# Two layers of attention and expert feed-forward on one core: the last layer norm of the first attention stage is finished by the next stage, and the end of the rotary attention runs in another order

## The chip, the cores and the metric

One core of one Trainium2 chip runs the whole program. The core has five engines that run side by side, each with its own instruction queue: PE (matrix products), DVE and POOL (elementwise work), ACT (activation functions and copies) and SP (which here only issues DMA transfers). They meet through semaphores. The metric is device time in microseconds, from one launch to its end; lower is better.

## The reference, cut to what matters

```python
# x: (8, 256, 256), context: (8, 256, 256)
x = x + tanh(g_xattn[0]) * L0_attention(layernorm(x), context)
x = x + tanh(g_ffn[0])   * L0_experts(layernorm(x))                 # 8 experts, the best 2 of each row
x = x + tanh(g_xattn[1]) * L1_rotary_attention(layernorm(x), context)
x = x + tanh(g_ffn[1])   * L1_experts(layernorm(x))                 # 8 experts, the best 1 of each row

def L0_attention(x, enc):
    x2 = layer_norm(x  + mha(x,  x,   x),   ln1_g, ln1_b)
    x4 = layer_norm(x2 + mha(x2, enc, enc), ln2_g, ln2_b)           # "the last norm of the attention"
    x5 = relu(x4 @ ff_w1 + ff_b1) @ ff_w2 + ff_b2
    return layer_norm(x4 + x5, ln3_g, ln3_b)
```

A layer norm here is (row - mean) / sqrt(variance + 1e-5), then times a gain and plus a shift of 256 numbers each. An expert layer sends each row to its expert (`relu(x @ W1[e] + b1[e]) @ W2[e] + b2[e]`) and weights the answer with the router's softmax.

## The kernel before

Rows are kept as 8 sequences of 256 rows, each as two tiles of 128 rows on 128 partitions. `X` holds the running value and `Y` the normed one; `here(Y, n)` is sequence n of it.

The program is a chain of stages. Each is a block in which every engine has a queue of its own, written out by hand; between two blocks all engines meet at a barrier (`stage_semaphores`), so a stage starts when the last engine of the one before is done. The stages that matter:

1. `attention_pipeline` (names `att_`): both attentions of layer 0 as one pipeline of M = 16 units, unit m being sequence m % 8 of the first attention for m < 8 and of the second for m >= 8. It runs in beats b, and a beat has 16 heads h. In beat b the heads of unit b are worked on; the output product of unit b - 1 (`project_out`, into `att_z`) comes at h = 12, and the layer norm of unit b - 2 is spread over the beat. So after the last unit's heads there are two more beats, b = 16 and b = 17, that hold only output products and norms. For the norm of unit m, DVE adds the product to `att_ybb` (`output_rows`) and takes mean and variance (`row_stats`), POOL finds the inverse root by 14 tiny instructions in a chain (`inverse_roots`), DVE scales (`norm`), and POOL multiplies with the gain and adds the shift (`gain_and_shift`). `att_ybb` is the residual plus the product's bias, made on POOL (`add_bias`). On POOL a beat is: roots, gain and shift of unit b - 2, then the bias of unit b - 1.
2. `feed_forward_and_experts` (`moe_`): the small feed-forward with its norm over 8 sequences, n = 0 to 7, and then 39 slots of 128 rows, each for one expert. PE runs `turn` (transposes of sequence n), `up_bank`, `down`. SP loads three rows of parameters first (`moe_b2r`, `moe_gain`, `moe_shift`), then the weights of 8 experts, 16 transfers of 1 MB.
3. `rotary_and_experts` (`out_`): the second layer's attention, in beats of 16 heads again (M = 8), then 23 slots of 128 rows for the experts with the best one of 8. The first 4 slots (`EARLY`) are filled from the first 6 sequences alone. For that the router works on a sequence as soon as it is normed: PE turns it (`turn_router`, task "t"), ACT copies it (`bring_router`), PE makes the logits (`logits`, "l"), DVE picks the expert (`top_expert`), PE counts ranks (`rank`, "n"), DVE makes destinations and weights, and POOL scatters the row numbers to DRAM (`scatter`, `ids<-out_numbered`). Then SP reads the list of a slot (`numbers`, `out_ids<-ids`), POOL gathers its rows (`rows_in`, `X<-rows` and `Y<-rows`), and PE turns and multiplies them (`turn_slot`, `up_slot` L1326, `down_slot` L1339). SP also writes each normed sequence to DRAM for these gathers (`keep_rows`), and `load_expert` loads 2 MB of an expert's weights; those of experts 6 and 7 need the place of the attention's operands.

Two of the PSUM banks of stage 3 are shared by all small products. `rotary_banks` gives the tasks the banks in turn, in the order in which PE meets them, and a task waits until the task two places before it has been read out. The end of the stage's attention, behind the last beat, is called the drain.

## Time and profile before

| | us |
|---|---|
| median of 3 runs | 1419.33 |
| lowest, highest | 1418.34, 1425.44 |
| the profiled execution's own time | 1420.58 |
| its span, first to last instruction | 1418.7 |
| PE busy in it | 1217.6 (86%) |
| DVE, ACT, POOL busy | 771.6, 560.9, 503.2 |

Times in the trace count from the first instruction of the span. The attention stage of layer 0 ends at about 466 us, the feed-forward stage runs from there to about 917 us, and the rotary stage to the end; its attention ends at about 1230 us. PE is the engine that is busy most, so the question at each place is what PE waits for.

### The profile page before, as it was taken

The page shows a single profiled execution, that of the slowest core. Times are in us where ns is not written, and L with a number is a line of the kernel's source. Part 1 is how long each engine was busy: PE and PEld are TensorE (multiplying, and loading weights), DVE is VectorE, ACT ScalarE, POOL GpSimd, SP SyncE. Part 2 cuts the span into 40 slices and gives each one's busy share as a digit, 9 for nine tenths or more (in the row PEclk, how much of TensorE's full clock was granted, in tenths as well). Part 3 has the DMA queues.
Part 4 walks back from the last instruction along what each step waited for, and adds up shares of the span by engine and source line. Part 5 has one row for each costly group of instructions (what it writes and reads, how often), then busy time and mean ns, then how long its engine had stood idle before and what let it go on. Part 6 is the DMA issues. An engine that isn't in the chain of part 4 may idle for free. (4 is left out here: it accounts for less than half of the span.)

```text
span 1418.7 us, 27157 instructions
## 1 busy us (share of the span) xinstructions
PE 1217.6 (86%) x8465; PEld 972.0 (69%) x8520; DVE 771.6 (54%) x2819; ACT 560.9 (40%) x1349; POOL 503.2 (35%) x909
## 2 busy tenths in 40 slices
PE   4598989999996899898999999755687888589996
PEld 3376666777753688788889888633455555489995
DVE  4676766777772277853412121147787876443321
ACT  2265555666664222233233333211354546133331
POOL 3344444453534235421000000156765543333331
PEclk9799999999999899999999999966799989799998
DMA  5767885657520771111111010166455587511110
GB/s 118 172 154 189 205 200 143 152 154 159 143 63 1 272 259 42 38 46 46 34 35 38 31 38 31 57 151 140 112 136 106 95 275 230 177 32 39 44 33 7
DMA packets 126293, 155.92 MB, mean 110 GB/s; under 512 B 19499, under 2 KB 111801, under 8 KB 121276
## 3 DMA queue, kind: packets, MB, share of 16 engines
q1 hardware_dynamic: 113736, 122.68, 34.2%
q0 software_dynamic: 9792, 27.30, 6.1%
q10 hardware_dynamic: 2624, 4.19, 1.0%
q8 instruction: 72, 1.18, 0.4%
q14 instruction: 69, 0.57, 0.2%
HBM read 104.17 MB, written 52.32 MB: 110 GB/s over the span
## 5 line engine op out<-in xcount | busy, mean ns | idle before, releaser
L761 DVE CUSTOM_DVE_ANT_0 att_masked_scores<-att_S,Bm 128x256 bf16<-128x256 f32 x512 | 192.4, 419 | 71.7 <-PE att_S L507 59.3
L644 ACT ACTIVATE att_PT<-att_T 128x512 f32<-128x512 f32 x256 | 151.4, 595 | 99.5 <-PE att_T L526 90.6
L2419 ACT ACTIVATE moe_hT<-moe_H,moe_b 128x128 f32<-128x128 f32 x312 | 89.2, 369 | 195.5 <-PE moe_H L2334 194.2
L2334 PE MATMUL moe_H<-moe_aT,ff_w 128*128 128x128 f32 x1248 | 147.7, 277 | 8.4 <-DVE ff_w L2617 8.4
L2334 PEld LDWEIGHTS moe_H<-moe_aT,ff_w 128*128 128x128 f32 x1248 | 146.7, 194 | 11.7 <-DVE ff_w L2617 9.9
L2346 PE MATMUL moe_Z<-moe_W,moe_hT 128*128 x624 | 142.6, 381 | 0.8 <-DVE moe_z L2624 0.8
L1615 POOL DMA_INDIRECT L_W<-yd,dest x32 | 31.3, 979 | 279.8 <-POOLq L52 271.2
L2346 PEld LDWEIGHTS moe_Z<-moe_W,moe_hT 128*128 128x128 f32 x624 | 115.4, 190 | 15.5 <-issue 1.2
L2624 DVE TENSOR_TENSOR moe_z<-moe_Z,moe_b 128x256 f32<-128x256 f32 x39 | 16.5, 424 | 200.7 <-PE moe_Z L2346 200.7
L507 PE MATMUL att_S<-L_KS,L_QS 96*128 96x256 bf16 x512 | 99.8, 277 | 26.9 <-DMA L_KS<-att_k_dram 21.7
L526 PE MATMUL att_T<-L_QS,L_KS 99*128 99x256 bf16 x512 | 98.7, 273 | 4.8 <-issue 2.3
L1790 DVE TENSOR_REDUCE out_mx<-out_S 128x2 f32<-128x512 f32 x128 | 85.8, 684 | 16.7 <-PE out_S L1207 11.8
L1507 ACT ACTIVATE X<-out_T,L_b 128x128 f32<-128x128 f32 x184 | 52.4, 370 | 97.5 <-PE out_T L1326 96.5
L1326 PEld LDWEIGHTS out_T<-out_xT,L_w1s 128*128 128x128 f32 x736 | 86.5, 194 | 4.4 <-issue 1.8
L1326 PE MATMUL out_T<-out_xT,L_w1s 128*128 128x128 f32 x736 | 87.3, 277 | 2.6 <-DVE L_w1s L1943 1.4
L1473 ACT ACTIVATE L_W<-out_T 128x512 f32<-128x512 f32 x128 | 72.5, 596 | 38.1 <-PE out_T L1225 31.9
L1339 PE MATMUL out_S<-L_W,X 128*128 x368 | 83.5, 380 | 2.5 <-DVE out_ys L1952 2.5
L524 PE MATMUL att_T<-BmT,identb 128*128 128x512 bf16 x201 | 77.0, 383 | 0.4
L526 PEld LDWEIGHTS att_T<-L_QS,L_KS 99*128 99x128 bf16 x512 | 50.6, 99 | 38.8 <-issue 0.8
L1207 PE MATMUL out_S<-L_W 97*128 97x256 bf16 x256 | 55.3, 305 | 25.2 <-DVE out_mx L1790 22.0
L1339 PEld LDWEIGHTS out_S<-L_W,X 128*128 128x128 f32 x368 | 68.1, 190 | 11.8 <-issue 3.5
L507 PEld LDWEIGHTS att_S<-L_KS,L_QS 96*128 96x128 bf16 x512 | 48.0, 98 | 40.6 <-DMA L_KS<-att_k_dram 23.2
(460 smaller groups left out, 2384.4 us busy)
## 6 DMA issues: line engine op xcount, KB each, us to landing
moe_W<-in_L_ffn_W SPq DMA_DIRECT2D x16, 1024.0 KB, 13.6
xd<-zero SPq DMA_DIRECT2D x12, 1280.0 KB
L_W<-in_L_ffn_W POOLq DMA_DIRECT2D x12, 1024.0 KB, 9.3
att_q_dram<-att_pq SPq DMA_DIRECT2D x16, 384.0 KB
att_k_dram<-att_pk SPq DMA_DIRECT2D x16, 384.0 KB
L_QS<-att_q_dram SPq DMA_DIRECT2D x16, 384.0 KB
L_KS<-att_k_dram SPq DMA_DIRECT2D x16, 384.0 KB
moe_xs<-xd SPq DMA_DIRECT2D x39, 128.0 KB
```

Source lines behind the costliest of these rows:

```text
L507: ins = nc.tensor.matmul(bankS[h % 2][:, u * SEQ:(u + 1) * SEQ], QS[0:ROWS, m % 3, h, u * P:(u + 1) * P], KS[0:ROWS, m % 3, h, :], start=T ...
L524: nc.tensor.matmul(dst[:, :], identb[:, :], masks[m // B][1][:, :], start=True, stop=False)
L526: ins = nc.tensor.matmul(dst[:, u * SEQ:(u + 1) * SEQ], KS[0:ROWS_ALL, m % 3, h, u * P:(u + 1) * P], QS[0:ROWS_ALL, m % 3, h, :], start=Fa ...
L644: nc.scalar.activation(PT[:, h % 8, :], bankT[h % 2][:, :], ACT.Exp).then_inc(exp_done, 1)
L761: ins = nc.vector.tensor_tensor_reduce(masked_scores[:, h % 2, u, :], bankS[h % 2][:, u * SEQ:(u + 1) * SEQ], masks[m // B][0][:, u * SEQ: ...
L1326: ins = nc.tensor.matmul(bankH[half][:, f * P:(f + 1) * P], matrix[:, cc, k * P:(k + 1) * P], xT[:, s % 2, cc * P:(cc + 1) * P], start=(cc ...
L1339: ins = nc.tensor.matmul(bankY[:, 0:D], eT[:, s % 2, f * P:(f + 1) * P], matrix[:, f, :], start=(f == 0), stop=(f == NF - 1))
L1473: nc.scalar.activation(PT[h % 8], bankT[h % 2][:, :], ACT.Exp).then_inc(exp_done, 1)
L1790: nc.vector.tensor_reduce(mx[:, m % 2, :, h:h + 1], bankS[h % 2][:, :].rearrange("p (u k) -> p u k", u=NU), AXX, ALU.max).then_inc(max_don ...
L2334: ins = nc.tensor.matmul(bankH[half][:, f * P:(f + 1) * P], w1s[:, cc, g * P:(g + 1) * P], xT[:, s % 2, cc * P:(cc + 1) * P], start=(cc == ...
L2346: ins = nc.tensor.matmul(bankZ[:, 0:D], eT[:, s % 2, f * P:(f + 1) * P], w2e[:, f, :], start=(f == 0), stop=(f == NF - 1))
L2419: ins = nc.scalar.activation(eT[:, s % 2, g * P:(g + 1) * P], bankH[half][:, f * P:(f + 1) * P], ACT.Relu, bias=b1[:, bass.ds(e * NF + g, 1)])
```

## The change

In `attention_pipeline` the beats stop after b = 16. The norm of the last unit (m = 15, sequence 7) isn't done there: DVE adds product and residual straight into `Y`, and the rest of the norm moves to the start of `feed_forward_and_experts`. In beat 16 POOL does the bias of unit 15 before the roots of unit 14. The feed-forward stage norms sequence 7 with its own helpers (`norm_rows` on DVE with the square root on ACT, whose function table is loaded for it) and a new `finish_last` on POOL; gain and shift come by two more transfers on SP, ahead of the others, into `yT`. Later readers of that sequence or of `yT` wait for `last_done`.

In `rotary_and_experts` the router's steps for sequence 5, the last of the early ones, move from the drain into the last beat; the drain's order changes on PE, DVE and POOL; and the loads of experts 6 and 7 move from ACT's queue to SP's, behind the four early lists.

```diff
@@ attention_pipeline
-        BEATS = range(-4, M + 2)
+        BEATS = range(-4, M + 1)
+        normed_here = lambda m: 0 <= m < M - 1
@@ POOL
+                if b == M:
+                    add_bias(M - 1)
-                if has(b - 2):
+                if normed_here(b - 2):
                     inverse_roots(nc, pool, t, moments, root_step, b - 2).then_inc(rooted, 1)
...
-                if has(b - 2):
+                if normed_here(b - 2):
                     gain_and_shift(b - 2)
-                if has(b - 1):
+                if has(b - 1) and b < M:
                     add_bias(b - 1)
@@ DVE, output_rows
-                nc.vector.tensor_tensor(z[:, m % 2, :, :], bank_of("z", m)[:, :].rearrange("p (u d) -> p u d", u=NU), ybb[:, :, :],
+                dst = z[:, m % 2, :, :] if m < M - 1 else here(Y, m)
+                nc.vector.tensor_tensor(dst, bank_of("z", m)[:, :].rearrange("p (u d) -> p u d", u=NU), ybb[:, :, :],
@@ rotary_tasks
+    more = LAST_BEAT.get(h, ()) if b == B - 1 else ()
...
-DRAIN_TASKS = ("t", 5), ("l", 5), ("o", 31), ("n", 5), ("a", 7), ("z", 7), ("t", 6), ("l", 6), ("t", 7), ("l", 7), ("n", 6), ("n", 7)
+LAST_BEAT = {11: (("t", 5),), 14: (("l", 5),)}
+DRAIN_TASKS = ("n", 5), ("o", 31), ("a", 7), ("z", 7), ("t", 6), ("l", 6), ("t", 7), ("l", 7), ("n", 6), ("n", 7)
@@ rotary_and_experts, SP
-            keep_rows(B - 2)
             sp.wait_ge(early_made, 1)
             sp.wait_ge(scattered[0], 16 * NU * EARLY_ONES)
             for s in range(EARLY):
                 numbers(s)
+            keep_rows(B - 2)
+            sp.wait_ge(s_ready, ALL)
+            sp.wait_ge(st_ready, ALL)
+            load_expert(sp, NE - 2)
+            sp.wait_ge(pv_done, QUADS * M + 2)
+            load_expert(sp, NE - 1)
             experts_here(NE - 2, NE)
@@ PE
+                    if b == M - 1 and h == 11:
+                        turn_router(EARLY_ONES - 1)
...
+                    if b == M - 1 and h == 14:
+                        logits(EARLY_ONES - 1)
...
-            turn_router(EARLY_ONES - 1)
             values(QUADS * M - 1)
-            logits(EARLY_ONES - 1)
+            rank(EARLY_ONES - 1)
             turn_out(QUADS * M - 1)
-            rank(EARLY_ONES - 1)
@@ ACT
+                    if b == M - 1 and h == 12:
+                        bring_router(EARLY_ONES - 1)
...
-            bring_router(EARLY_ONES - 1)
-            act.wait_ge(s_ready, ALL)
-            act.wait_ge(st_ready, ALL)
-            load_expert(act, NE - 2)
             outputs(QUADS * M - 1)
-            act.wait_ge(pv_done, QUADS * M + 2)
-            load_expert(act, NE - 1)
@@ POOL
+            scatter(EARLY_ONES - 1)
             inverse_roots(nc, pool, t, moments, root_step, M - 2).then_inc(rooted, 1)
-            scatter(EARLY_ONES - 1)
+            rows_in(0)
             inverse_roots(nc, pool, t, moments, root_step, M - 1).then_inc(rooted, 1)
-            for s in range(EARLY):
+            for s in range(1, EARLY):
                 rows_in(s)
@@ DVE
+                    if b == M - 1 and h == 15:
+                        top_expert(EARLY_ONES - 1)
+                        centre(EARLY_ONES - 1)
...
             row_stats(M - 2)
-            top_expert(EARLY_ONES - 1)
-            centre(EARLY_ONES - 1)
+            destinations(EARLY_ONES - 1)
             normalise(QUADS * M - 1)
-            destinations(EARLY_ONES - 1)
             expert_weights(EARLY_ONES - 1)
             early_table()
+            output_rows(M - 1)
             norm(M - 2)
-            output_rows(M - 1)
@@ feed_forward_and_experts
+            for i, k in enumerate(("last_gain", "last_shift")):
+                sp.dma_start(yT[:, i, :], rows_in[k].partition_broadcast(P)).then_inc(last_in, 16)
@@ turn(n)
+                if n == B - 1:
+                    pe.wait_ge(last_done, 1)
@@ bring_router(n)
+                if n == 0:
+                    act.wait_ge(last_done, 1)
@@ ACT
             bring(0)
+            norm_root(nc, act, t1, step1, root1, 0)
@@ POOL
+            def finish_last():
+                pool.wait_ge(last_in, 32)
+                pool.wait_ge(last_normed, 1)
+                nc.gpsimd.tensor_tensor(here(Y, B - 1), here(Y, B - 1), rows_of(yT[:, 0, :]), ALU.mult).then_inc(last_scaled, 1)
+                pool.wait_ge(last_scaled, 1)
+                nc.gpsimd.tensor_tensor(here(Y, B - 1), here(Y, B - 1), rows_of(yT[:, 1, :]), ALU.add).then_inc(last_done, 1)
...
             add_bias(0)
+            finish_last()
@@ DVE
+            norm_rows(nc, dve, here(Y, B - 1), here(Y, B - 1), t1, step1, root1, 0, waited).then_inc(last_normed, 1)
             then(routing_constants(nc, rt))
```

The first place is POOL's queue where the attention stage of layer 0 ends. Before, behind gain and shift of unit 14 (`att_z`, `Y`), it held this:

```order
L711 TENSOR_TENSOR att_z<-att_z,L_gain 128x512
L713 TENSOR_TENSOR Y<-att_z,L_shift 128x512
L707 TENSOR_TENSOR att_ybb<-Y,L_bo 128x512
L134 TENSOR_SCALAR att_ve<-att_mv 128x2
L135 TENSOR_SCALAR att_guess<-att_ve 128x2
L138 TENSOR_TENSOR att_a<-att_guess 128x2
L139 TENSOR_TENSOR att_b<-att_a,att_ve 128x2
L140 TENSOR_SCALAR att_c<-att_b 128x2
L141 TENSOR_TENSOR att_r<-att_guess,att_c 128x2
```

Now the block's end (the branch) follows at once, and the new work stands behind the first bias of the next stage; `moe_yT` holds the gain and then the shift of the last unit:

```order
L712 TENSOR_TENSOR att_z<-att_z,L_gain 128x512
L714 TENSOR_TENSOR Y<-att_z,L_shift 128x512
L346 UNCONDITIONAL_BRANCH
L51 ISA x2
L2475 UNCONDITIONAL_BRANCH
L2502 IOTA moe_slot_no 1x27
L2479 TENSOR_TENSOR Y<-Y,moe_b2r 128x512
L2484 TENSOR_TENSOR Y<-Y,moe_yT 128x512
L2486 TENSOR_TENSOR Y<-Y,moe_yT 128x512
```

What went from POOL's end of the stage is the bias of unit 15 (it stands earlier now), its 14 root instructions and its gain and shift.

The second place is PE's queue from head 11 of the last rotary beat. L1225 are the transposed scores of a head (`out_T`), L1238 the values of four heads (`out_O`), L1246 turns of their outputs, L1267 the output product of sequence 6, L1277 the router's turn and L1289 its logits. Before:

```order
L1246 MATMUL out_B<-ident,out_OTS 128x128 x2
L1225 MATMUL out_T<-L_W 128x256 x2
L1267 MATMUL out_A<-L_wo,out_aT 128x256 x4
L1225 MATMUL out_T<-L_W 128x256 x2
L1238 MATMUL out_O<-L_W,L_w1s 32x256 x8
L1225 MATMUL out_T<-L_W 128x256 x4
L1246 MATMUL out_B<-ident,out_OTS 128x128 x2
L1277 MATMUL out_A<-ident,Y 128x128 x4
L1238 MATMUL out_O<-L_W,L_w1s 32x256 x8
L1289 MATMUL out_B<-L_wg,out_yT 128x8 x4
```

And of the change, where these lines are 11 higher:

```order
L1288 MATMUL out_B<-ident,Y 128x128 x4
L1257 MATMUL out_A<-ident,out_OTS 128x128 x2
L1236 MATMUL out_T<-L_W 128x256 x2
L1278 MATMUL out_B<-L_wo,out_aT 128x256 x4
L1236 MATMUL out_T<-L_W 128x256 x2
L1249 MATMUL out_O<-L_W,L_w1s 32x256 x8
L1236 MATMUL out_T<-L_W 128x256 x2
L1300 MATMUL out_A<-L_wg,out_yT 128x8 x4
L1236 MATMUL out_T<-L_W 128x256 x2
L1257 MATMUL out_B<-ident,out_OTS 128x128 x2
L1249 MATMUL out_O<-L_W,L_w1s 32x256 x8
```

The router's turn stands ahead of the output product now, and both write bank B, so the product waits until ACT has copied the turned rows; the logits stand ahead of the last values.

The third place is SP's queue behind the fourth early list (`out_ids<-ids`). Before, only sequence 7 was written to DRAM there (`rows<-Y`, `rows<-X`) ahead of the later lists. Now it is this, with sequence 6, four weight transfers of 1 MB and then sequence 7:

```order
L1102 DMA out_ids<-ids 128x2
L1091 DMA rows<-Y 128x2x256
L1091 DMA rows<-X 128x2x256
L1053 DMA L_W<-in_L_ffn_W 128x2x1024
L1054 DMA L_W<-in_L_ffn_W 128x8x256
L1053 DMA L_W<-in_L_ffn_W 128x2x1024
L1054 DMA L_W<-in_L_ffn_W 128x8x256
L1091 DMA rows<-Y 128x2x256
L1091 DMA rows<-X 128x2x256
```

What moved here is the rows of sequence 6, which stood ahead of the lists, and the weights, which stood on ACT.

## Rows read from the trace of the kernel before

**Rows 1.** The page's head.
```profile
span 1418.7 us, 27157 instructions
```
**Rows 2.** Timeline of PE at the end of layer 0's attention: start us, us, group.
```profile
450.68 1.99 PE L568 MATMUL att_B<-L_wo,att_aT 128*128 128x256 f32 x8 [0.75 <-ACT att_aT L618]
467.07 1.09 PE L2257 MATMUL moe_T<-ident,Y 128*128 128x128 f32 x4 [14.39 <-PEq L52]
468.90 8.85 PE L2269 MATMUL moe_H<-moe_aT,ff_w 128*128 128x256 f32 x32 [0.75 <-ACT moe_aT L2389]
...
484.94 7.07 PE L2269 MATMUL moe_H<-moe_aT,ff_w 128*128 128x256 f32 x32
```
**Rows 3.** Timeline of POOL over the same stretch.
```profile
447.72 0.21 POOL L134 TENSOR_SCALAR att_ve<-att_mv 128x2 f32<-128x2 f32 x1 [4.85 <-DVE att_mv L118]
...
451.34 0.20 POOL L141 TENSOR_TENSOR att_r<-att_r,att_c 128x2 f32<-128x2 f32 x1
...
453.74 1.26 POOL L713 TENSOR_TENSOR Y<-att_z,L_shift 128x512 f32<-128x512 f32 x1
...
464.28 1.26 POOL L713 TENSOR_TENSOR Y<-att_z,L_shift 128x512 f32<-128x512 f32 x1
467.05 0.17 POOL L2476 IOTA moe_slot_no<- 1x27 f32 x1 [1.51 <-POOLq L52]
472.71 1.27 POOL L2460 TENSOR_TENSOR Y<-Y,moe_b2r 128x512 f32<-128x512 f32 x1 [5.50 <-DMA moe_shift<-in_L_xattn_ln_b]
```
**Rows 4.** Timeline of DVE over the same stretch.
```profile
443.46 0.69 DVE L802 TENSOR_TENSOR att_z<-att_B,att_ybb 128x512 f32<-128x512 f32 x1 [1.72 <-PE att_B L568]
...
456.42 0.69 DVE L802 TENSOR_TENSOR att_z<-att_B,att_ybb 128x512 f32<-128x512 f32 x1 [4.10 <-POOL att_ybb L707]
...
485.32 0.69 DVE L2508 TENSOR_TENSOR moe_z<-moe_Z,Y 128x512 f32<-128x512 f32 x1 [17.25 <-PE moe_Z L2282]
```
**Rows 5.** Busy time by stretch; the number behind POOL's is PE's granted clock.
```profile
455.00:455.50 0.50, 0.00 (x0) 0.00 (x0) 0.00 (x0) 0.00 (x0) 0.50 (x1) 0.77 0.00 0
...
472.00:472.50 0.50, 0.50 (x3) 0.42 (x2) 0.00 (x0) 0.00 (x0) 0.00 (x0) 0.66 0.88 248
```
**Rows 6.** Timeline of ACT: its first copy for the feed-forward stage's router.
```profile
499.83 0.60 ACT L2404 ACTIVATE moe_yT<-moe_R 128x512 f32<-128x512 f32 x1 [2.75 <-PE moe_R L2292]
```
**Rows 7.** Chain that ended last, in the rotary drain: start us, us, what.
```profile
1205.25 1.00 PE out_B L1289 x8
...
1210.57 1.03 POOL ids L1635
...
1211.90 7.30 DMA ids<-out_numbered,out_place
...
1220.21 3.21 DMA out_ids<-ids
...
1224.25 4.06 DMA X<-rows,out_ids
1228.36 0.69 PE out_S L1311 x2
...
1231.50 4.59 PE out_T L1326 x32
```
**Rows 8.** Timeline of PE in the last rotary beat and behind it.
```profile
1199.57 1.89 PE L1267 MATMUL out_A<-L_wo,out_aT 128*128 128x256 f32 x8
...
1204.18 1.07 PE L1238 MATMUL out_O<-L_W,L_w1s 128*32 128x256 f32 x16
```
**Rows 9.** Timeline of ACT in that beat: the exponentials of heads 10 to 12.
```profile
1198.69 1.68 ACT L1473 ACTIVATE L_W<-out_T 128x512 f32<-128x512 f32 x3
```
**Rows 10.** DMA issues of 1184 to 1197 us: transfers, median us to landing.
```profile
ids<-out_numbered,out_place POOLq DMA_INDIRECT x2, 4.6
```
**Rows 11.** DMA issues of 1198 to 1209 us, in the same columns.
```profile
L_W<-in_L_ffn_W ACTq DMA_DIRECT2D x4, 1024.0 KB, 11.7
```
**Rows 12.** Timeline of POOL: the gather of slot 4.
```profile
1256.40 1.28 POOL L1649 DMA_INDIRECT X<-rows,out_ids  x1 [3.30 <-DMA out<-X,out_ids]
```

More of the change, by code:

```diff
@@ L831, in _ @@
                         queries(b + 3)
-                    if h == 1 and has(b - 2):
+                    if h == 1 and normed_here(b - 2):
                         row_stats(b - 2)
@@ L841, in _ @@
                         max_columns(b + 1)
-                    if h == 9 and has(b - 2):
+                    if h == 9 and normed_here(b - 2):
                         norm(b - 2)
@@ L870, in rotary_tasks @@
         return [t for t in LAST_FILL.get(h, ())]
+    more = LAST_BEAT.get(h, ()) if b == B - 1 else ()
     units = [(k, QUADS * b + d if k == "o" else b + d) for k, d in TASKS.get(h, ()) + ROUTE_TASKS.get(h, ())]
     last = {"o": QUADS * B, "t": EARLY_SEQUENCES1 - 1, "l": EARLY_SEQUENCES1 - 1, "n": EARLY_SEQUENCES1 - 1}
-    return [(k, n) for k, n in units if 0 <= n < last.get(k, B)]
+    return more + tuple((k, n) for k, n in units if 0 <= n < last.get(k, B))
 ROUTE_TASKS = {1: (("l", -3),), 5: (("n", -3),), 13: (("t", -2),)}
-DRAIN_TASKS = ("t", 5), ("l", 5), ("o", 31), ("n", 5), ("a", 7), ("z", 7), ("t", 6), ("l", 6), ("t", 7), ("l", 7), ("n", 6), ("n", 7)
+LAST_BEAT = {11: (("t", 5),), 14: (("l", 5),)}
+DRAIN_TASKS = ("n", 5), ("o", 31), ("a", 7), ("z", 7), ("t", 6), ("l", 6), ("t", 7), ("l", 7), ("n", 6), ("n", 7)
 def rotary_banks():
@@ L2212, in feed_forward_and_experts @@
         w1_ready, x_loaded, y_stored = sem("w1_ready"), sem("x_loaded"), pair("y_stored")
+        last_in, last_normed, last_scaled, last_done = sem("last_in"), sem("last_normed"), sem("last_scaled"), sem("last_done")
         block = ctx.enter_context(nc.Block())
@@ L2429, in _ @@
                 if n >= 1:
-                    norm_root(nc, act, t1, step1, root1, n - 1)
+                    norm_root(nc, act, t1, step1, root1, n)
                 for j in range(1, HB):
@@ L2440, in _ @@
             bring_router(B - 2)
-            norm_root(nc, act, t1, step1, root1, B - 1)
+            norm_root(nc, act, t1, step1, root1, B)
             for s in range(SLOTS):
@@ L2509, in rows @@
                 dve.wait_ge(z_out, n + 1)
-                norm_rows(nc, dve, z, z, t1, step1, root1, n, waited).then_inc(normed, 1)
+                norm_rows(nc, dve, z, z, t1, step1, root1, n + 1, waited).then_inc(normed, 1)
             def new_rows(n):
@@ L2708, in flamingo @@
             feed_forward_and_experts(nc, "moe", c, ff, {"b2r": a["L0_xattn_ff_b2"], "gain": a["L0_xattn_ln3_g"],
-                                     "shift": a["L0_xattn_ln3_b"]}, X, Y, L, xd0, yd0, dest, weight, gate_x0, gate_f0,
+                                     "shift": a["L0_xattn_ln3_b"],
+                                     "last_gain": a["L0_xattn_ln2_g"], "last_shift": a["L0_xattn_ln2_b"]}, X, Y, L, xd0, yd0, dest, weight, gate_x0, gate_f0,
                                      a["L0_ffn_W1"], a["L0_ffn_W2"], a["c_L0_ffn_b1"], a["L0_ffn_b2"])
```

## The prediction

> **What bounds the kernel now.** I read three views: the timelines of PE, POOL and DVE where the first attention stage ends, the chain that ended last in the rotary drain, and the sizes of DMA landings beside both. The span is 1418.7 us [rows 1]; the sum below is made against the profiled execution's own 1420.58 us, which is 1.25 above the median of 1419.33.
>
> At the first place PE is through with the attention at 450.68 + 1.99 = 452.67 and starts again at 467.07, after 14.39 us of nothing [rows 2]. The reader should see who is last: POOL, whose gain and shift of unit 15 end at 464.28 + 1.26 = 465.54, and 1.5 us later every engine is in the next stage [rows 3]. Behind 467.07 PE works without a gap through the feed-forward's sequences, so what the barrier gives up, the whole rest of the program gets, as long as the next stage's start is not made slower.
>
> At the second place the chain shows a row of handovers with PE idle: logits at 1205.25, scatter issued at 1210.57 and 1211.90, 7.30 us until it has landed, the list read by SP (3.21), the gather (4.06), PE's turn of slot 0 at 1228.36 and its first product at 1231.50 [rows 7]. From there PE is the chain to the end, so the end moves with that product.
>
> **The first part, piece by piece.** Removed from the stage's end are unit 15's statistics, 14 roots, scaling, gain and shift, and ahead of them the bias. The bias was what DVE waited for at 456.42, though the product was there at 452.67 [rows 2, 4]. Now POOL does it before the roots of unit 14. It needs the sum of unit 14, ready at 443.46 + 0.69 = 444.15 [rows 4], and takes 1.27 us; the roots of unit 14 started at 447.72 after 4.85 us of waiting [rows 3], so it hides wholly in that wait (cover 2.3 us; without it it would cost 1.27). DVE adds at about 452.7 and is done at 453.4. The last thing of the stage is then POOL's shift of unit 14, which ended at 453.74 + 1.26 = 455.00 [rows 3]; its roots (447.72 to 451.54) and what follows don't move. So the end comes at 455.00 instead of 465.54: **-10.54 us**, and PE starts at about 456.5.
>
> Added to the next stage: DVE norms sequence 7 first, some 5 us with the square root and a load of ACT's table, while it had nothing to add until 485.32, 18 us after the start [rows 4]. The table load isn't new, it stood later in the same queue. On SP two small transfers stand ahead; three such ones put POOL's first bias at 472.71, 5.6 us after the start [rows 3], so I expect it 1 to 2 us later, against those 18 us. On POOL gain and shift (2.6 us) follow the first bias, done some 11 us after the start. The first to wait for `last_done` is ACT's router copy, which came at 499.83, 32.8 us after the start [rows 6]. All this costs 0. What is queued behind it on POOL is gain and shift of sequence 0, due some 23 us after the start; if `last_done` came 22 us late, ACT, and through it PE, would wait.
>
> The clock: PE's first products in the new stage took 8.85 us where the same 32 took 7.07 later [rows 2]. The granted clock fell from 2.4 to 1.2 GHz between 455.0 and 455.5, 2.6 us after PE's last product, and rose at about 472.3 [rows 5]. PE now restarts at 456.5, still behind that fall, so I take the same price again: 0. The bounds are -2.3 us if the clock doesn't fall (8.85 - 7.07 and the same on the turns, 0.5) and +1 if it rises later.
>
> **The second part.** PE turns sequence 5 for the router at head 11, ahead of the output product. The product of sequence 6, at 1199.57 before [rows 8], now waits for ACT's copy, which comes behind the exponentials of heads 10 to 12 (1198.69 + 1.68 = 1200.37) [rows 9] and takes 0.6: it starts at about 1201.0, 1.4 us late. The logits (1.00 [rows 7]) stand ahead of the last head too. So the last values, at 1204.18 before [rows 8], come 2.4 us later. In exchange DVE picks the expert meanwhile; but now the statistics of sequence 6 and the rank behind the values stand in the way of the destinations. Going through DVE's queue, I get the weights of sequence 5 about 0.8 us later than before (bounds: 1 earlier, 2 later), and the scatter's second issue at 1212.7.
>
> Then the gain: the scatter of 1211.90 took 7.30 us to land [rows 7], in a stretch in which the 4 MB of experts 6 and 7 were arriving. The scatter before it but one took 4.6 [rows 10]. With the weights issued later I take 4.6: -2.7 (bound: 0). The list and the gather of slot 0 follow by the same steps, so its rows arrive 1.9 us earlier, at 1226.5. But POOL now does the roots of sequence 7 behind that gather, and PE wants that sequence's turn before its first slot product: roots take 3.8 us [rows 3], behind the gather's issue at 1222.3 to 1223.9, then DVE's scaling and the turn. The product starts at about 1230.4 by that path instead of 1231.3: **-0.9 us**. Bounds: -2.0 if the roots don't decide, +4 from the rival below.
>
> [...]
>
> **Sum.** 1420.58 - 10.54 - 0.9 = 1409.1 for a profiled run, 1.25 less against the median: **1408 us**, 0.8% faster.
>
> **Rivals.** (A) *The drain gives back.* The weights now leave SP at about 1222.5, just as POOL issues the gathers of slots 0 to 3 (256 KB each). The measured sign that this hurts is the scatter: 7.30 us beside such weights, 4.6 without [rows 7, 10]. A gather stretched by the same 2.7 us puts slot 0's product at 1232 and lets PE wait up to 2 more for slots 1 and 2: +3 against my sum's -0.9, so 1411.8. For it speaks that PE stands right behind; against it that the weights' bulk comes after slot 0's gather. The Trainium skill, DMA: Bandwidth & Descriptors, section on queues, rings and completion order, says each DMA engine goes round between its queues a packet at a time, which is this rival's mechanism; and under "Issuing engines are not separate DMA queues" that SP, ACT and POOL all feed the same 16 engines, by which ACT to SP alone brings nothing. By that rule slot 0's gather shares from its first packet; the scatter's row agrees in kind, and nothing before shows gathers beside weights.
>
> (B) *More than forecast.* The clock stays up over the short gap and the roots don't decide: 1419.33 - 10.5 - 2.3 - 2.0 = 1404.5. Against it is the fall at 455.0 to 455.5 [rows 5].
>
> (C) *The barrier doesn't move*, because something else than POOL ended it, or the next stage's start is late by as much (the change doesn't do what it says): 1418.4. The three rows of POOL, DVE and PE leave little room; SP's waits at the end are for transfers long done.
>
> (D) *Slower.* SP now waits until 4 MB have landed before it writes sequence 7, which slot 4's gather at 1256.40 needs [rows 12]. The loads took 11.7 us [rows 11]; from 1222.5 that is 1234, the rows landed by 1240, some 15 us in time. Only if they took over 26 us would PE wait, and only beyond 45 would it be slower than before by over 0.5%: 1427 and more.
>
> **Chances and range.** Forecast 0.58 (its own range 1405.5 to 1410.5), A 0.18, B 0.12, C 0.08, D 0.04. What a measurement of this kernel can tell from no change is about 0.5%, 7.1 us: faster is below 1412.2. The forecast, B and four fifths of A lie there, and some of C between: 0.86 faster, 0.10 same, 0.04 slower. The range 1403.5 to 1413 leaves out C, D and the far ends of A and B.
>
> **What the new profile would show.** Right: POOL's last work of the attention stage is the shift of unit 14, DVE's addition into `Y` no later than 453.5, PE's gap there near 3.9 us instead of 14.4, and the first feed-forward products again near 8.9 us. In the drain: the output product of sequence 6 behind ACT's router copy, the scatter's landing near 4.6, slot 0's turn about 13 us earlier in the trace than before (10.5 of it from the first part). Wrong: a gap on PE ahead of `turn` of sequence 7 or behind ACT's first router copy; gathers of slots 0 to 3 over 6 us to landing with PE waiting; PE waiting for weights or rows at slot 4. Most likely to make the forecast wrong is the drain, whose queues all changed at once.

## The result

| | us |
|---|---|
| median of this kernel, 8 runs (lowest, highest) | 1408.08 (1403.39, 1411.90) |
| median of the kernel before, 8 runs (lowest, highest) | 1420.23 (1416.50, 1427.94) |
| ratio, with its 95% interval | 0.9899 [0.9879, 0.992] |
| profiled execution of this kernel: own time, span | 1403.39, 1401.5 |

The kernel is 1% faster, by 12.15 us between the medians. The forecast was 1408.0 and 11.4 us of gain.

The timeline of POOL at the end of layer 0's attention in the changed kernel (start us, us, group) answers to [rows 3]:

```profile
439.81 1.27 POOL L708 TENSOR_TENSOR att_ybb<-Y,L_bo 128x512 f32<-128x512 f32 x1 [1.42 <-DVE att_z L806]
443.25 0.21 POOL L134 TENSOR_SCALAR att_ve<-att_mv 128x2 f32<-128x2 f32 x1 [2.16 <-DVE att_mv L118]
...
449.25 1.27 POOL L714 TENSOR_TENSOR Y<-att_z,L_shift 128x512 f32<-128x512 f32 x1
452.04 0.17 POOL L2502 IOTA moe_slot_no<- 1x27 f32 x1 [1.51 <-POOLq L52]
459.81 1.27 POOL L2479 TENSOR_TENSOR Y<-Y,moe_b2r 128x512 f32<-128x512 f32 x1 [7.61 <-DMA moe_shift<-in_L_xattn_ln_b]
...
462.38 1.27 POOL L2486 TENSOR_TENSOR Y<-Y,moe_yT 128x512 f32<-128x512 f32 x1
```

The bias of unit 15 stands at 439.81, inside POOL's wait for the row sums of unit 14. The shift of unit 14 is now the stage's last work, ending at 450.52, and again 1.5 us pass until POOL is in the next stage. Behind the first bias there, the two operations of `finish_last` end at 463.65.

The timeline of PE in the same stretch answers to [rows 2]:

```profile
442.10 1.07 PE L540 MATMUL att_O<-att_PT,att_V 128*32 128x256 f32 x16 [0.52 <-ACT att_PT L645]
...
446.20 3.58 PE L569 MATMUL att_B<-L_wo,att_aT 128*128 128x256 f32 x8 [0.75 <-ACT att_aT L619]
452.06 0.63 PE L2273 MATMUL moe_T<-ident,Y 128*128 128x128 f32 x4 [2.28 <-PEq L52]
453.44 8.56 PE L2285 MATMUL moe_H<-moe_aT,ff_w 128*128 128x256 f32 x32 [0.75 <-ACT moe_aT L2405]
...
462.27 7.07 PE L2298 MATMUL moe_Z<-ff_w,moe_hT 128*128 128x256 f32 x32
```

PE stands idle for 2.28 us there instead of 14.39. Its last product of the attention took 3.58 us where 1.99 in [rows 2]: the same eight matrix products at the other clock, as the busy time by stretch shows (the number behind POOL's is the granted clock, 0.50 being 1.2 GHz and 1.00 being 2.4):

```profile
447.00:449.00 2.00, 2.00 (x6) 1.55 (x6) 0.74 (x2) 0.00 (x0) 1.15 (x2) 0.50 0.00 0
450.10:452.10 2.00, 0.04 (x1) 0.07 (x2) 0.51 (x2) 0.00 (x0) 0.49 (x2) 1.00 0.00 0
453.50:456.00 2.50, 2.50 (x6) 2.05 (x7) 0.90 (x6) 1.39 (x2) 0.00 (x0) 0.50 0.47 136
460.00:462.00 2.00, 2.00 (x12) 1.72 (x11) 0.00 (x0) 0.84 (x2) 2.00 (x2) 1.00 0.95 388
```

The rows of DVE and ACT show what became of unit 15:

```profile
449.87 0.69 DVE L806 TENSOR_TENSOR Y<-att_B,att_ybb 128x512 f32<-128x512 f32 x1 [2.04 <-issue]
...
455.92 0.73 DVE L89 TENSOR_SCALAR Y<-Y,moe_amv,moe_arstd 128x256 f32<-128x256 f32 x2
...
469.56 0.69 DVE L2535 TENSOR_TENSOR moe_z<-moe_Z,Y 128x512 f32<-128x512 f32 x1 [12.45 <-PE moe_Z L2298]
```
```profile
484.07 0.60 ACT L2422 ACTIVATE moe_yT<-moe_R 128x512 f32<-128x512 f32 x1 [4.17 <-PE moe_R L2308]
```

DVE's part of the norm is done at 456.65 and then DVE waits 12.45 us for PE anyway; ACT's first router copy at 484.07 waits for PE's turn and not for `last_done`, which had come 20 us earlier.

The chain that ended last, in the rotary drain, answers to [rows 7]:

```profile
1185.28 1.96 PE out_B L1278 x8
...
1195.31 0.97 POOL ids L1644
1196.59 4.46 DMA ids<-out_numbered,out_place
1202.06 1.74 DMA out_ids<-ids
...
1204.62 5.57 DMA X<-rows,out_ids
1210.24 0.69 PE out_S L1322 x2
1210.93 1.51 PE out_B L1300 x8
1212.44 0.95 PE out_A L1288 x4
1213.38 5.57 PE out_T L1337 x32
```

The scatter lands in 4.46 us instead of 7.30, the gather in 5.57 instead of 4.06, and slot 0's turn is 18.12 us earlier in the trace than in [rows 7].

**Two marks that take the noise out.** One execution differs from the next by up to ten us, more than the drain is worth. In fourteen profiles the last value product of the attention (`att_O`, mark A) starts anywhere from 440.03 to 447.29 us, and from the second product of the feed-forward stage to the values of quad 29 (mark B, the third value product from the end of the rotary attention; 1197.26 before, 1181.52 in the changed kernel) it takes 716.2 to 722.2 us; no edit here changes PE's work in either stretch. Of the 18.12 us at slot 0's turn, 4.47 lie ahead of A (446.57 before, 442.10 in the changed kernel) and are no work of the change. Measured from A, a landmark at the barrier repeats within 0.1 us where the same engine ends the stage. Measured from B it repeats less well: the two profiles of the changed kernel (changed and e9) are 1.6 us apart at slot 0's turn and 1.3 at the end, so a single profile tells no edit of under some 1.3 us in the drain. The table has these distances in us, starts read from the timelines; "end" is the span less B. The medians come from five series; that of the kernel before was 1420.23 beside the changed kernel, 1419.84 beside e1 to e4, 1418.21 beside e5 to e8, 1417.95 beside e9 to e11 and 1418.16 beside e12, and each ratio is to the one of its own series.

| kernel | median | ratio to before | A: POOL's end | A: first turn | A: `moe_Z` | B: list | B: slot 0's turn | B: its product | B: end |
|---|---|---|---|---|---|---|---|---|---|
| before | 1420.23 | | 18.97 | 20.50 | 31.46 | 22.95 | 31.10 | 34.03 | 221.44 |
| changed | 1408.08 | 0.9899 [0.9879, 0.992] | 8.42 | 9.96 | 20.17 | 20.54 | 28.72 | 31.65 | 219.98 |
| e9, changed again | 1404.09 | 0.9899 [0.9881, 0.9917] | 8.41 | 9.95 | 20.16 | 20.29 | 27.08 | 30.01 | 218.69 |
| e1, boundary alone | 1407.73 | 0.9918 [0.989, 0.9947] | 8.39 | 9.92 | 20.80 | 22.50 | 29.70 | 32.63 | 221.21 |
| e2, drain alone | 1416.20 | 0.9979 [0.9959, 1.0] | 18.91 | 20.44 | 32.61 | 19.99 | 27.21 | 30.14 | 220.01 |
| e3, bias alone | 1417.64 | 0.999 [0.9967, 1.0012] | 16.76 | 18.29 | 29.93 | 22.51 | 29.70 | 32.63 | 221.86 |
| e4, 7 idle products | 1412.38 | 0.9952 [0.9933, 0.9972] | 17.66 | 19.19 | 30.68 | 20.13 | 27.43 | 30.36 | 219.74 |
| e10, 14 idle products | 1423.11 | 1.0045 [1.0031, 1.006] | 27.06 | 28.59 | 39.72 | 20.13 | 27.29 | 30.22 | 219.92 |
| e5, loads on ACT | 1405.77 | 0.9906 [0.989, 0.9922] | 8.44 | 10.07 | 20.35 | 23.00 | 29.59 | 32.52 | 220.94 |
| e6, router late | 1406.92 | 0.991 [0.9888, 0.9932] | 8.44 | 9.96 | 21.79 | 19.53 | 26.06 | 29.85 | 219.12 |
| e7, loads later | 1407.71 | 0.992 [0.9905, 0.9936] | 8.40 | 9.92 | 21.04 | 20.13 | 26.93 | 29.87 | 218.58 |
| e8, gather behind roots | 1410.27 | 0.9951 [0.9932, 0.997] | 8.42 | 9.95 | 21.11 | 19.91 | 34.65 | 37.59 | 224.86 |
| e11, e6 with e7 | 1401.69 | 0.9881 [0.9865, 0.9897] | 8.44 | 9.96 | 21.13 | 19.52 | 26.09 | 29.84 | 219.02 |
| e12, product first | 1401.54 | 0.9876 [0.9859, 0.9892] | 8.43 | 9.96 | 21.76 | 19.27 | 25.82 | 27.87 | 219.09 |

### The profile page after: what moved, and what is told of

It is laid out like the page before. It is cut to its first block and busy times, and to the rows that moved or that the text cites. A ratio compares the mean times of both kernels' runs of the same rounds, so it can differ in the third digit from the quotient of the medians.

```text
span 1401.5 us, 27155 instructions
## 1 busy us (share of the span) xinstructions
PE 1219.7 (87%) x8465; PEld 973.2 (69%) x8520; DVE 769.8 (55%) x2825; ACT 560.6 (40%) x1350; POOL 500.7 (36%) x895
```

## The experiments

**e1 to e4: the two parts apart.** e1 is the kernel before with all hunks of `attention_pipeline` and `feed_forward_and_experts`, e2 the kernel before with all hunks of the rotary stage; of each the diff shows the head.

```diff
@@ e1
-        BEATS = range(-4, M + 2)
+        BEATS = range(-4, M + 1)
+        normed_here = lambda m: 0 <= m < M - 1
...
@@ e2
-DRAIN_TASKS = ("t", 5), ("l", 5), ("o", 31), ("n", 5), ("a", 7), ("z", 7), ("t", 6), ("l", 6), ("t", 7), ("l", 7), ("n", 6), ("n", 7)
+LAST_BEAT = {11: (("t", 5),), 14: (("l", 5),)}
+DRAIN_TASKS = ("n", 5), ("o", 31), ("a", 7), ("z", 7), ("t", 6), ("l", 6), ("t", 7), ("l", 7), ("n", 6), ("n", 7)
...
```

> This is the kernel before with the boundary edits alone: the norm of unit 15 done by the feed-forward program, its bias ahead of the roots of unit 14, the drain of the rotary attention as it was. The theory of the prediction: POOL's last work in the attention is what the block waits for, and it ends 10.5 us earlier, so the kernel is 10.5 us faster than before (bounds -12.8 to -9.5), and from the second turn of the feed-forward program to the end every landmark keeps that distance (a little more, by some 0.8 us, since the first turn ran at full clock in the changed kernel). Rival, the gain of the changed kernel is mostly the drain's: this kernel is then under 8 us faster. Rival, given back on the way (the bias of unit 0 came 7.8 us after the program's start in the changed kernel, where 5.7 us before): under 9 us.

> This is the kernel before with the drain edits alone, the boundary as it was. By the steps of the prediction it is 0.9 us faster than before; by the landmarks of the changed kernel's profile, where 0.5 us of a slower product was inside, 1.4 us. The scatter of sequence 5 lands after about 4.5 us instead of 7.3, the last values come about 2 us later, the first gather lands after about 5.5 us instead of 4.1. Rival, the drain gives all back and the change's gain is the boundary's alone: 0 to +2 us.

Both came out, but for one landmark of e2: from its first gather's issue to PE's turn it is 4.66 us, where landing after about 5.5 was expected. e1 has the first turn 9.92 us behind A (20.50 before) and its drain is that of before (221.21 against 221.44); its median is 12.1 us under before's 1419.84 of that series. e2 has the boundary of before (20.44) and the end 220.01 behind B, 1.5 us less than the mean 221.50 of the three profiles with the old drain. Its median is 3.6 us lower, and its ratio's interval reaches 1.

e3 is the kernel before with one edit on POOL:

```diff
+                if b == M:
+                    add_bias(M - 1)
                 if has(b - 2):
                     inverse_roots(nc, pool, t, moments, root_step, b - 2).then_inc(rooted, 1)
...
-                if has(b - 1):
+                if has(b - 1) and b < M:
                     add_bias(b - 1)
```

> This is the kernel before with one edit: POOL adds the bias of unit 15 ahead of the roots of unit 14, everything else as it was, so the norm of unit 15 stays in the attention. In the rows before, the roots of unit 15 could not start until the row sums, which waited for the product's sum with the bias, which POOL made only after gain and shift of unit 14 (455.05), and the sum came at 456.42 with 4.10 us of idle. With the bias early the sum is made right behind the product, about 3 to 4 us earlier, but POOL itself is free for the roots of unit 15 only at the end of the shift of unit 14 (455.0, with the bias now ahead of it), where before it started them at 458.3. So the theory gives 3.2 us faster (bounds -4 to -2), and the other 7 us of the boundary's gain belong to the work that left POOL. Rival, the bias is what matters and the moved norm gives little: 7 us or more. Rival, POOL's order there does not matter: 0.

POOL's end came 2.2 us nearer to A (18.97 to 16.76), at the low end of the bounds. I had let the roots start when POOL came free, and in this execution they started later. The timelines of POOL and PE in e3:

```profile
450.68 1.26 POOL L713 TENSOR_TENSOR Y<-att_z,L_shift 128x512 f32<-128x512 f32 x1
453.06 0.21 POOL L134 TENSOR_SCALAR att_ve<-att_mv 128x2 f32<-128x2 f32 x1 [1.12 <-DVE att_mv L118]
```
```profile
447.65 3.47 PE L568 MATMUL att_B<-L_wo,att_aT 128*128 128x256 f32 x8 [0.74 <-ACT att_aT L618]
```

POOL waits 1.12 us more, for DVE's sums of unit 15, which wait for PE's product, and that took 3.47 us here where 1.99 in [rows 2]. With a product of 1.99 us the sums would stand 1.48 us sooner and the wait would be gone: by that estimate the early bias is worth 3.3 us, which is the 3.2 expected. So with the norm still there the early bias is worth 2.2 us as measured and some 3.3 where the product is fast, and the work that left the stage the other 7.2 to 8.3 of 10.5. The median (2.2 us lower) doesn't tell it from nothing; the landmark does.

e4, and later e10, are the changed kernel with idle work behind POOL's queue, products into a tile that nobody reads any more (7 of them in e4, 14 in e10):

```diff
+            for i in range(7):
+                pool.wait_ge(gained, M - 1 + i)
+                nc.gpsimd.tensor_tensor(z[:, 1, :, :], z[:, 1, :, :], rows_of(w_of(M - 1)["gain"]), ALU.mult).then_inc(gained, 1)
```

> This is the changed kernel with seven more products of z and gain (128x512 each, chained, 1.27 us each by POOL's rows in this stage) at the end of POOL's queue in the attention; they change nothing that is read later. They put POOL's end 8.9 to 9.4 us back. The theory, that the next program starts when the last engine of the attention ends and that POOL is that engine: the time rises by 8.0 to 9.4 us over the changed kernel (its own product ends 0.7 us before POOL's last work, so nearly all shows), and by another 0.8 us if the turn of the feed-forward program falls back to the half clock. Rival, the next program starts by something else (loads of weights, the output product): under 3 us.

At the boundary it came out to a tenth: POOL's end and the first turn both 9.2 us further from A. The median did not: 4.3 us above that of the changed kernel, which was measured in another series. (By the ratios, each to the kernel before in its own series, it is 0.9952 against 0.9899, some 7.5 us, and the two intervals leave room for 9.2.) So I gave twice the dose and ran the changed kernel beside it.

> This is the changed kernel itself once more, as a control beside the next two. Four kernels with its boundary, and three with its drain, put its gain at 11.5 us between the last value product of the attention and the second product of the feed-forward program, and 1.6 us from the start of the values of quad 29 to the end. So 13 us less than the kernel before if the stages between cost the same on the average (their spread from one execution to the next is some 3 to 6 us), and 10.5 to 14 by the median. Rival: part of the boundary's gain is given back by the stages behind it in most executions, and the median is 9 us or less.

> This is the changed kernel with fourteen idle products at the end of POOL's queue in the attention instead of the seven of the earlier run, 18.6 us. With seven, the profiled execution showed all of it at the boundary (POOL's end 9.2 us and the first turn 9.2 us later behind the last value product), yet the median over its runs was only 4.3 us above the changed kernel's and the mean 5.4. Theory, POOL's end moves the next program one for one, and the smaller median was the spread of the other stages: first turn 28.4 to 28.7 us behind the last value product (9.96 without), and the median 16.5 to 20 us above the changed kernel's of this same call. Rival, a longer idle stretch of PE gives some of it back later (a higher clock in the stages behind): the turn is late by the same but the median only 9 to 15 us above, and the granted clock of the whole is above that of the control.

Timelines of POOL and PE in e10:

```profile
448.41 18.68 POOL L734 TENSOR_TENSOR att_z<-att_z,L_gain 128x512 f32<-128x512 f32 x14
468.60 0.17 POOL L2505 IOTA moe_slot_no<- 1x27 f32 x1 [1.51 <-POOLq L52]
```
```profile
444.13 1.99 PE L569 MATMUL att_B<-L_wo,att_aT 128*128 128x256 f32 x8 [0.75 <-ACT att_aT L619]
468.62 1.09 PE L2276 MATMUL moe_T<-ident,Y 128*128 128x128 f32 x4 [22.49 <-PEq L52]
```

The first turn is 28.59 us behind A, 18.6 more than without, and the median is 19.0 above that of e9 in the same series. No sign of anything given back later; e4's small median is laid to the comparison of two series, and that was not settled further. e9 itself gave a median 13.9 us under before's (1417.95), with the same ratio as the first comparison.

**e5 to e8: the drain, edit by edit.** All are the changed kernel less one thing, or with one thing more. e5 puts the loads back on ACT.

```diff
@@ SP
-            sp.wait_ge(s_ready, ALL)
-            sp.wait_ge(st_ready, ALL)
-            load_expert(sp, NE - 2)
-            sp.wait_ge(pv_done, QUADS * M + 2)
-            load_expert(sp, NE - 1)
@@ ACT
+            act.wait_ge(s_ready, ALL)
+            act.wait_ge(st_ready, ALL)
+            load_expert(act, NE - 2)
             outputs(QUADS * M - 1)
+            act.wait_ge(pv_done, QUADS * M + 2)
+            load_expert(act, NE - 1)
```

> This is the changed kernel with the loads of experts 6 and 7 back on ACT at their old place, ahead of the last values, nothing else undone. All distances are from the start of the values of quad 29. In five profiles so far the list of the early slots was read 22.5 to 22.95 us behind them with the drain of before and 20.0 to 20.5 with the new one, and the scatter of sequence 5 landed in about 6.9 to 7.3 us and about 4.5. Theory of the prediction, the 4 MB beside the scatter cost it the 2.7 us: the list is read at 22.7 to 23.3 and the first product of slot 0 comes 1.6 to 2.7 us later than in the changed kernel (30.1 to 31.7 there), the end 1 to 2 us later. Rival, the earlier list comes from the earlier router steps or from SP having the list ahead of the rows of sequence 6, and not from the weights: list at 20.0 to 20.6, no loss.

The chain of e5, and then the same rows of e9:

```profile
1200.13 6.89 DMA ids<-out_numbered,out_place
1208.06 1.73 DMA out_ids<-ids
...
1210.61 3.99 DMA X<-rows,out_ids
```
```profile
1199.97 4.20 DMA ids<-out_numbered,out_place
1205.20 1.73 DMA out_ids<-ids
```

The scatter takes 6.89 us beside the loads and 4.20 without them, the list is read at 23.00 behind B and the product comes at 32.52: the early loads are the cause of the long scatter. The gather takes 3.99 us here, with no weights beside it. The end is 220.94, 1.3 later than the mean 219.67 of the five profiles with the changed drain (changed, e9, e2, e4, e10) and 0.9 behind the latest of them. Again only landmarks tell; the median is no higher. The Trainium skill, DMA: Bandwidth & Descriptors, section "Issuing engines are not separate DMA queues", says that DMAs started by the scalar, sync or gpsimd engine run on the same 16 DMA engines and interleave, whichever started them. No run here tries the engine alone: e5 changes it together with the moment of the issue, 8.4 to 10.5 us behind B instead of 24.8 to 28.4.

e6 moves the router steps of sequence 5 back into the drain (task lists, PE, ACT and DVE as before the change, the order of DVE's norms too), and keeps the rest.

```diff
-LAST_BEAT = {11: (("t", 5),), 14: (("l", 5),)}
-DRAIN_TASKS = ("n", 5), ("o", 31), ("a", 7), ("z", 7), ("t", 6), ("l", 6), ("t", 7), ("l", 7), ("n", 6), ("n", 7)
+LAST_BEAT = {}
+DRAIN_TASKS = ("t", 5), ("l", 5), ("o", 31), ("n", 5), ("a", 7), ("z", 7), ("t", 6), ("l", 6), ("t", 7), ("l", 7), ("n", 6), ("n", 7)
```

> This is the changed kernel with the router's steps of sequence 5 (turn, logits, highest expert, centring) back in the drain and the row norm order of before; the weights stay on SP behind the list, POOL's scatter and first gather as changed. Theory: early router steps bring nothing to the scatter, which went out 0.4 us later with them (15.07 against 14.67 behind the start of the values of quad 29), and they make the last values 2.06 us later. So here the second scatter goes out at 14.7, the list is read at 19.6 to 20.1, and the end is 0 to 0.8 us earlier than in the changed kernel. Rival, the norms decide: the turn of sequence 6's router waits in PE's queue ahead of the turn of slot 0 and with it in the old place the end is the same within 0.3. Rival, the early steps do bring something: the scatter later than 15.1 and the end 0.5 to 1.5 us later.

The scatter's second issue is at 14.57 behind B (15.07 with the early steps), the last values at 6.93 (8.98), the list at 19.53, slot 0's turn at 26.06, the end at 219.12: 0.6 under the mean, but inside the spread of the five (218.69 to 220.01). So the early router steps bring nothing, and the list is 0.5 to 1.0 us sooner without them; that the end gains by it isn't shown. The product gained little, 29.85; the timeline of PE in e6 says why:

```profile
1213.74 0.69 PE L1322 MATMUL out_S<-ident,X 128*128 128x128 f32 x2 [4.65 <-DMA X<-rows,out_ids]
1214.22 1.72 PE L1300 MATMUL out_B<-L_wg,out_yT 128*128 128x8 f32 x8
1216.62 1.12 PE L1288 MATMUL out_A<-ident,Y 128*128 128x128 f32 x4 [0.68 <-DVE Y L151]
```

Sequence 7's turn now waits for DVE's norm, which waits for POOL's roots behind the gather. That is the mechanism of my prediction, met at 28.94 us behind B. Further on the same timeline has a second wait that goes back to these roots: slot 1's gather leaves at 28.64, behind them, takes 7.61 us, and PE waits 1.29 us for its rows.

e7 has one more wait on SP:

```diff
+            sp.wait_ge(x_loaded[0], 16)
             sp.wait_ge(s_ready, ALL)
             sp.wait_ge(st_ready, ALL)
             load_expert(sp, NE - 2)
```

> This is the changed kernel in which SP also waits for the landing of slot 0's rows before it issues the loads of experts 6 and 7 (about 3.5 us later). Theory: slot 0's rows took 5.6, 4.7 and 4.7 us from issue to PE's turn beside the moved weights where 4.1 without them, so here the turn comes 0.6 to 1.0 us sooner after the gather's issue (distance 4.0 to 4.2), slots 1 to 3 keep it, and the end is 0.5 to 1 us earlier if the rows of sequence 7 still stand in time. Rival: the longer distance has another cause (the rows of sequence 6 now beside the gather, issued by SP 1.2 us behind it): distance 4.6 to 5.7 as before and no gain.

From the gather's issue to PE's turn it is 4.23 us, where the five profiles with the changed drain have 4.23 to 5.62 (e9 the shortest). The end is 218.58, 1.1 under their mean but only 0.1 under e9's, so a gain isn't shown. In four of the five slot 0's gather took 0.4 to 1.4 us longer than here, which fits loads that lengthen it; but e6, where the loads leave SP as early as in the five, has 3.97. The stronger sign is in e8.

e8 has all four gathers behind both roots:

```diff
-            rows_in(0)
             inverse_roots(nc, pool, t, moments, root_step, M - 1).then_inc(rooted, 1)
-            for s in range(1, EARLY):
+            for s in range(EARLY):
```

> This is the changed kernel with the first gather of rows behind the roots of sequence 7 on POOL, as it was in the kernel before. The prediction held that roots of sequence 7 behind the gather would decide PE's start and eat most of the drain's gain. In the profiles the norm's product of sequence 7 came just in time. Theory from them: without this edit the gather waits for the roots, that is until about 28.5 us behind the start of the values of quad 29 (where 22.6 to 23.1 with it), so slot 0's turn is at 32.5 to 33.5 where 27.2 to 28.7, and the end 4 to 5.5 us later than in the changed kernel, 2 to 4 us worse than the drain of before. Rival, as the prediction put it: roots decide either way, and the end is later by 1 us at most.

The end came as the theory had it, slot 0's turn later than it had (34.65, where 32.5 to 33.5 was expected). The chain of e8 goes through the roots,

```profile
1199.07 0.76 DVE out_stats L114 x2
1201.04 1.06 POOL out_b L139
1205.75 6.80 DMA X<-rows,out_ids
1212.59 0.69 PE out_S L1322 x2
```

the gather leaves at 27.81 behind B, 3.1 us behind the first of the loads, and takes 6.80, where 3.97 to 4.11 in the profiles of before, e1, e3 and e5, with no weights beside it, and of e6 (from issue to PE's turn). The end is 224.86, 5.2 over the changed drain and 3.4 over the old one. Without `rows_in(0)` ahead of the roots the rest of the drain's edits would be a loss.

**e11 and e12: what could be mended.** e11 is e6 and e7 together.

> This is the changed kernel with the two edits together that each gained at the drain: router steps of sequence 5 back in the drain (end 0.8 us earlier by the profile), and the loads of experts 6 and 7 behind the landing of slot 0's rows (1.3 us earlier). If they add, the end is 217.5 to 218.2 us behind the start of the values of quad 29 (219.9 with the changed kernel, 221.5 with the drain of before), so 1.7 to 2.4 us faster than the changed kernel by landmarks, which the median can hardly tell from it. Rival: both free the same slack (slot 0's rows sooner, while its product and slots 1 to 3 wait for the rows of slot 1 and the results' sums), and the end is 218.5 to 219.2.

The rival: 219.02, with the product at 29.84. e12 is e11 with PE sent past the floor that e6 and e11 wait at (e7 comes 0.04 us behind it and doesn't wait):

```diff
@@ PE
-            turn_router(M - 1)
             up_slot(0)
+            turn_router(M - 1)
@@ ACT
             bring_slot(0)
-            bring_router(M - 1)
             hidden_slot(0)
+            bring_router(M - 1)
```

> This is the kernel with both drain edits mended (router steps of sequence 5 late, loads behind slot 0's rows), in which PE also multiplies slot 0 by its first weights ahead of the turn of the router rows of sequence 7, and ACT brings them in that order. In the three kernels where slot 0's rows came earliest, slot 0's first product stood at 29.84 to 29.87 us behind the start of the values of quad 29, whether its rows were turned at 26.1 or at 26.9, and the turn of sequence 7 ahead of it waited for the norm, which waits for POOL's roots of sequence 7 behind the gather. Theory: those roots are the floor; past them the product starts 1.2 to 1.5 us behind slot 0's turn, at 27.2 to 27.8, and the end comes 0.5 to 2 us earlier than the 219.0 of the kernel with both edits. Rival: slots 1 to 3 are held by their own rows, whose gathers stand behind the same roots (slot 1's rows were turned at 36.1 with 1.05 us of idle time), so the product is early and the end the same within 0.4. Second rival: the later router of sequence 7 makes the late list late, the turn of slot 4 comes after 66 us and the end is later than 219.4.

The first rival. The timeline of PE in e12:

```profile
1212.03 0.69 PE L1323 MATMUL out_S<-ident,X 128*128 128x128 f32 x2 [4.40 <-DMA X<-rows,out_ids]
1212.51 1.72 PE L1301 MATMUL out_B<-L_wg,out_yT 128*128 128x8 f32 x8
1214.08 6.34 PE L1338 MATMUL out_T<-out_xT,L_w1s 128*128 128x128 f32 x32
1220.25 0.60 PE L1289 MATMUL out_A<-ident,Y 128*128 128x128 f32 x4
1221.76 0.44 PE L1323 MATMUL out_S<-ident,X 128*128 128x128 f32 x2 [0.91 <-DMA X<-rows,out_ids]
```

The product is 2 us earlier (27.87), but takes 6.34 us where 5.18 in e11: the granted clock is 0.50 (1.2 GHz) in both until about 33 us behind B, so the earlier product does more of its work at the low clock. Then PE waits 0.91 for slot 1's rows (1.05 in e11), whose gather stands behind the roots of sequence 7. The end is the same, 219.09. The medians of e11 (1401.69) and e12 (1401.54) are the lowest of all, but e9's 1404.09 is inside their spread (1399.38 to 1408.74 for e11): by the landmark they are 0.6 us ahead of the changed drain's mean and inside its spread, so neither is shown faster than the changed kernel.

## Why the prediction was right, step by step

- **POOL ends the stage, 10.54 us earlier.** Right within a hundredth: 18.97 to 8.42 us behind A, and PE's first turn 20.50 to 9.96. e4 and e10 show the barrier following POOL's end one for one.
- **The bias is hidden.** Right: it lies in POOL's wait, and roots and shift of unit 14 keep their distance to A.
- **DVE's addition by 453.5, PE's gap 3.9.** Half right. As a distance to A, the forecast end was 6.9 us, and it is 6.88 in all five profiles with the early bias in which the product ran at 2.4 GHz (e4, e7, e8, e10, e11); PE's gap is 3.83 to 3.87 in the three of them without idle products. In the changed kernel's it is 8.46, since the product there ran at 1.2 GHz. The stage was then ended by DVE (450.56) and POOL (450.52) together. So the next us off POOL's queue would bring nothing in such an execution. In e5 DVE ended the stage at 8.57, and the first turn came at 10.07.
- **The next stage pays nothing.** Right: `last_done` 11.6 us after the first turn (11 forecast), POOL's first bias at 7.8 instead of 5.6 us, and nobody waits for either.
- **The clock: 0, bounds -2.3 and +1.** Inside the bounds, not at 0. From A to `moe_Z` it is 31.46 and 32.61 us with the old boundary (before, e2) and 20.16 to 21.79, mean 20.9, in nine profiles with the new one: 11.1 saved, 0.6 more than the barrier's part. That 0.6 is not clear of the spread: from the first turn to `moe_Z` it is 10.96 and 12.17 us with the old boundary and 10.2 to 11.8 with the new.
- **The drain's issue times.** The output product of sequence 6 came 1.45 us later behind B (1.4 forecast), the last values 2.06 (2.4), the scatter 0.4 (0.8).
- **The scatter lands in 4.6 instead of 7.30.** Right, 4.46, and by the loads (e5).
- **The product of slot 0 gains only 0.9, since the roots of sequence 7 decide.** This step failed. The forecast product was at 1230.4, 33.1 us behind B (against 1231.3 before, which is the timeline's 1231.29 and not the 1231.50 of the chain in [rows 7]). It stands at 32.63 to 34.03 with the old drain and at 30.01 to 31.65 with the changed one: 2.6 between the means. In the five profiles of the changed drain PE came to the turn of sequence 7 at 29.1 to 30.8, behind slot 0's turn and the logits, and the norm was done 0.2 to 1.1 us sooner; the roots bind there at 28.94, as e6 and e11 show, where slot 0's rows came a us earlier. The mis-sized term stands ahead of the roots: I had slot 0's gather issued at 1222.3, 25.0 behind B, and it left at 22.6 to 23.1. Of the 2.3 us between them, on the mean, the list's read is 1.5: it took 3.21 us in [rows 7], which I carried over, and 1.73 or 1.74 in the eight other profiles whose chain shows it, e3 with the old drain among them.
- **"The end moves with that product."** This failed too. Of the 2.6 us the end keeps 1.8 (221.50 to 219.67), and in e12 2 us more on the product left the end where it was. The roots of sequence 7 do decide, but by slot 1's rows, whose gather waits for them. The chain of e9:

```profile
1212.84 0.20 POOL out_r L141
1213.55 7.25 DMA X<-rows,out_ids
1220.85 0.44 PE out_S L1322 x2
```

In seven profiles (e2, e6, e7, e9 to e12) slot 1's gather leaves 28.4 to 28.6 us behind B, takes 7.0 to 7.8 and keeps PE waiting 0.7 to 1.3 us. In the other two of the changed drain (changed, e4) slot 0's product came or ended late enough to cover it.
- **Rival A** had the right mechanism, and less of it reached PE than it had. Slot 0's gather, issued 2.2 us ahead of the first load, took 0.1 to 1.5 us more than the 4.11 of before where A had 2.7; a gather issued in the midst of the loads took 2.7 to 3.7 more (slot 0's in e8, slot 1's in the seven above). PE waited up to 1.3 us for slot 1 where A had up to 2 for slots 1 and 2. So what I had named as a sign of being wrong, gathers over 6 us with PE waiting, did show, and the drain still gained. **C** and **D** fell: sequence 7's rows were issued 15 us ahead of slot 4's gather, which kept nobody waiting.

The terms measured are 11.1 and 1.8, together 12.9, against 11.4 forecast and 12.15 and 13.9 between the medians. That the forecast's 1408.0 met the median of 1408.08 is luck in good part: the drain gave twice its 0.9, and before's own median came out 0.9 us higher in that comparison than in the runs it was built on.

## What to carry to other kernels

At a barrier, ask which engine's last work ends it and whether that work must be done in this stage: eleven us of tiny dependent operations cost nothing on the other side, where the engines had 12 us to wait. Work off the last engine pays one for one only until the next engine is last, here 1.5 us further, and no further where the clock was low. And when single terms are smaller than the spread between runs, measure each from a mark just ahead of it in the same execution, and take more than one profile of the same kernel to see how far such a distance repeats. Last, a time read from one trace, as the list's 3.21 us here, can be that execution's own.

## What the runs showed that I had not expected

- The clock can be low ahead of the barrier. The last output product took 1.99 us in some executions and 3.16 to 3.68 in others of the same code (3.58 in the changed kernel, at a granted clock of 0.50, 1.2 GHz, from 447 to 449 us, while PE had been idle for no longer than 0.75 us at a time just before). What sets it off was not tried.
- A scatter of 256 row numbers, 1 KB, takes 3.9 to 4.5 us to land with the loads later (e2, e4, e7, e9, e10, the changed kernel) and 6.8 to 7.3 beside 4 MB of loads (before, e3, e5).
- Four gathers of 256 KB behind one another beside the same loads: slot 1's takes 7.0 to 7.8 us (e2, e6, e7, e9 to e12), slot 0's 4.0 to 5.6 from issue to PE's turn.
